# A fused model of six layers on one core: four edits to the order and the size of the work

## The reference

```
def routed_and_shared(x, cond):                  # 4096 tokens
    shared = (silu(x @ sw1.T) * (x @ sw3.T)) @ sw2.T          # hidden size 1024
    s = sigmoid(x @ router_w.T + cond @ router_t_w.T)         # 8 experts
    pick the 2 best of s + router_bias; gates = their s, normed to a sum of 1
    routed = sum over the 2: gate * gelu(x @ rw1[e].T) @ rw2[e].T   # hidden size 256
    return (shared + routed) / 3
def expert_ffn(y):                               # one expert of 8 for each batch,
    e = argmax(gelu(y[last token] @ Wp1 + bp1) @ Wp2 + bp2)   # chosen by its last row
    return y + 0.3 * ((gelu(y @ W1[e] + b1[e]) @ W2[e] + b2[e]) @ Wo + bo)   # hidden 1024
def hashed_ffn(x, token_ids, shift_state):       # 16 experts of 256 tokens by hash
    xk, xr = x mixed with the row before it
    return sigmoid(xr @ w_recept) * (relu(xk @ w_key[e]) ** 2 @ w_value[e])
def recurrent(x):                                # 32 steps, c = f * c + i * g
    gates from x @ w and c @ u; out = tanh(x @ wo + c_last @ uo + bo)

x = x + expert_ffn(routed_and_shared(x, cond))
x = x + recurrent(hashed_ffn(x, token_ids, cond))
```

## Time and profile before

| | us |
|---|---|
| runs (3) | 2507.08, 2508.03, 2508.68 |
| median | 2508.03 |
| profiled execution | 2510.33 |
| its span in the trace | 2508.7 |
| mean granted clock of TensorE | 0.994 |

### The profile page before, as it was taken

How to read it: one execution, slowest core, us unless ns; L and a number is a source line. 1 busy time by engine, 2 the same in 40 slices (tenths; PEclk the granted TensorE clock), 3 DMA queues, 4 the chain that set the end, 5 groups by cost and what they waited for, 6 DMA issues and landing times. The chain is left out here.

```text
span 2508.7 us, 40888 instructions
## 1 busy us (share of the span) xinstructions
PE 2456.5 (98%) x12556; PEld 2048.4 (82%) x12557; DVE 1148.4 (46%) x1766; ACT 896.8 (36%) x1454; POOL 548.5 (22%) x492
## 2 busy tenths in 40 slices
PE   8999999999999899999999989999999999999999
PEld 4778888888899688878888879989978888888877
DVE  5555555325343344334434357667643333333356
ACT  2233333226555222222222246666542222222234
POOL 1100000002222276656657510000001111111100
PEclk9999999999999899999999999999999999999999
DMA  7698898317466443363344265665641011110035
GB/s 283 212 344 305 300 319 318 136 48 264 151 241 222 167 122 110 116 248 108 110 154 150 84 240 218 237 241 215 234 155 42 26 34 29 29 34 25 25 99 186
DMA packets 134500, 412.81 MB, mean 165 GB/s; under 512 B 30115, under 2 KB 32611, under 8 KB 117778
## 3 DMA queue, kind: packets, MB, share of 16 engines
q1 hardware_dynamic: 107186, 315.25, 35.7%
q0 software_dynamic: 18736, 60.80, 8.0%
q10 hardware_dynamic: 8496, 35.69, 3.7%
HBM read 558.71 MB, written 144.80 MB: 280 GB/s over the span
## 5 line engine op out<-in xcount | busy, mean ns | idle before, releaser
L99 PE MATMUL s_g<-wx_hi,s_x_hi 128*128 128x512 f32 x512 | 203.4, 397 | 2.3 <-DVE s_x_lo L2268 1.6
L101 PE MATMUL s_g<-wx_hi,s_x_lo 128*128 128x512 f32 x512 | 200.2, 391 | 0.0
L100 PE MATMUL s_g<-wx_lo,s_x_hi 128*128 128x512 f32 x512 | 199.5, 390 | 0.0
L1981 DVE TENSOR_TENSOR s_w_lo<-s_w_raw,s_w_hi 128x1024 fp32r<-128x1024 f32 x124 | 146.5, 1222 | 75.2 <-ACT s_w_hi L1910 73.6
L99 PE MATMUL s_g<-s_u,s_c_hi 128*128 128x512 f32 x384 | 152.8, 398 | 1.6 <-PEq L1795 1.6
L101 PE MATMUL s_g<-s_u,s_c_lo 128*128 128x512 f32 x384 | 149.9, 390 | 0.0
L100 PE MATMUL s_g<-s_u,s_c_hi 128*128 128x512 f32 x384 | 149.5, 389 | 0.0
L99 PE MATMUL s_h_ps<-s_x_hi,s_w_hi 128*128 128x256 f32 x512 | 144.9, 283 | 1.7 <-DVE s_x_lo L2006 1.7
L100 PE MATMUL s_h_ps<-s_x_lo,s_w_hi 128*128 128x256 f32 x512 | 144.9, 283 | 0.0
L101 PE MATMUL s_h_ps<-s_x_hi,s_w_lo 128*128 128x256 f32 x512 | 144.9, 283 | 0.0
L2167 POOL DMA_INDIRECT s_y<-mid_hash_out,first_rec x32 | 31.5, 983 | 476.8 <-DMA mid_hash_out<-s_o 392.5
(11 more groups left out here) (401 smaller groups left out, 6913.9 us busy)
## 6 DMA issues: line engine op xcount, KB each, us to landing
s_half<-mid_w ACTq DMA_DIRECT2D x124, 2048.0 KB
s_w_raw<-in_w SPq DMA_DIRECT2D x64, 512.0 KB, 6.4
mid_w<-s_x_grp SPq DMA_DIRECT2D x32, 1024.0 KB, 5.6
mid_w<-s_pool_b SPq DMA_DIRECT2D x32, 1024.0 KB, 4.9
s_half<-mid_w SPq DMA_DIRECT2D x32, 1024.0 KB
s_w_raw<-in_w2h SPq DMA_DIRECT2D x16, 2048.0 KB, 7.5
s_w_raw<-in_w1h SPq DMA_DIRECT2D x15, 2048.0 KB, 7.5
mid_routed<-s_o_sb SPq DMA_DIRECT2D x72, 256.0 KB, 2.0
```

What stands on the lines that cost most here:

```text
L99: pe.matmul(out, a_hi, w_hi, start=first, stop=False, skip_group_check=True)
L100: pe.matmul(out, a_hi, w_lo, start=False, stop=False, skip_group_check=True)
L101: return pe.matmul(out, a_lo, w_hi, start=False, stop=last, skip_group_check=True)
L1981: dve.tensor_tensor(lo[:, c], raw[:, c], hi[:, c], ALU.subtract).then_inc(S[name + "_lo"], 1)
```

## The change

1. `places()` in the shared stage's DVE list moves from behind the parts that follow group 0 to ahead of the last of them.
2. `EARLY` is 4 instead of 5. ACT and DVE split the down weights of four experts at the end of the shared stage; the fifth is loaded and split in the routed stage, so that `LATE` has eight pieces, from step 2 to step 9, instead of six, from step 2 to 7. Each expert from number 5 on has its pieces two steps later.
3. `RT` is 71 instead of 72: the lists of 8 experts with 8192 places in all never need more than 71 whole tiles. All that runs over routed tiles is one shorter: gathers, matmuls, stores, and the lists of `places()` and `one_hots`. `CHECKED`, the counts at which the stage sees whether experts are through, ends with 71.
4. In the expert stage `combine` of batch j moves in DVE's list from ahead of `h_add(1)` of batch j - 1 to behind `h_lo(1)`. PE's list stays.

```
-RT = 2 * NTOK // P + ER
+RT = 2 * NTOK // P + ER - 1
-EARLY = 5
+EARLY = 4
 ...
@@ stage_shared, ACT
                     if g == G - 1:
                         routed_hi(m)
-                        if m == TG - 1:
-                            routed_hi(EARLY - 1)
@@ stage_shared, DVE
             x_lo(1)
             for point in range(HC, POINTS):
+                if point == POINTS - 1:
+                    places()
                 if is_part(0, point):
                     part_lo(part_at(0, point))
-            places()
@@ stage_ffn, POOL, gather
                 if isinstance(i, int) and i == 0:
                     for m in range(4):
-                        pool.wait_ge(R[f"o_out{m}"], 16 * RT // 4)
+                        pool.wait_ge(R[f"o_out{m}"], 16 * ((RT + 3 - m) // 4))
@@ stage_ffn, DVE
             software_pipeline(dve, NB, [
-                (2, z_add), (1, h_add(0)), (2, part_lo(z_lo, tz_ps, z_hi, "z_hi", "z_lo")), (0, combine), (1, h_add(1)),
-                (1, h_lo(0)), (2, x1_), (1, h_lo(1)), (3, hashed_lo(0, 2)),
+                (2, z_add), (1, h_add(0)), (2, part_lo(z_lo, tz_ps, z_hi, "z_hi", "z_lo")), (1, h_add(1)),
+                (1, h_lo(0)), (2, x1_), (1, h_lo(1)), (0, combine), (3, hashed_lo(0, 2)),
                 (3, xr_lo_), (2, last_mix), (3, hashed_lo(2, DC)), (0, make_shift),
                 (0, y_lo_)], 2)
```

More of the change, by code:

```diff
@@ L156, in stage_shared @@
                  "w_hi w_lo ones sig dve pe_rank ~rec_out zeroed ~zero_out ~route ~tile_in0 ~tile_in1 ~tile_in2 ~tile_in3 "
-                 "rw_in0 rw_in1 rw_in2 rw_in3 rw_in4 rw_hi "
+                 "rw_in0 rw_in1 rw_in2 rw_in3 rw_hi "
                  "xt_in xt_hi xt_lo gu silu hmul h_hi h_lo mm2 o_ready ~o_out0 ~o_out1 one_hot list_ps list_sum hash_members hash_total_read hash_rank_read "
@@ L848, in stage_routed @@
         ps = lambda n, s, t=FP32: ctx.enter_context(nc.psum_tensor("s2_" + n, s, t))
-        S = sems(nc, ctx, "s2_", "w_in5 w_in6 w_in7 w_hi w_lo wo_in0 wo_in1 wo_hi wo_lo tx x_hi x_lo mm1 "
+        S = sems(nc, ctx, "s2_", "w_in4 w_in5 w_in6 w_in7 w_hi w_lo wo_in0 wo_in1 wo_hi wo_lo tx x_hi x_lo mm1 "
                  "gelu th h_hi h_lo mm2 o_ready ~o_out0 ~o_out1 ~o_out2 ~o_out3 "
```

## The result

The changed kernel takes 2527.28 us at the median of four runs (2526.12 to 2531.51), the kernel before 2508.35 beside it: the ratio is 1.0079, 95% interval [1.0067, 1.0091], or 18.9 us slower. The direction was forecast, the size was not: 2516.0 was predicted, with a range that ended at 2523. The profiled execution took 2526.12 us with a span of 2524.5, 15.8 more than the span of before.

A forecast was written before the change was run, and what follows sets the result against it. TensorE, busy 98% of the span, was taken as the bound. Terms -1.7 - 1.2 - 1.7 - 3.4 + 4.0 + 10.0 - 4.8 + 6.8 gave +8.0 us, so 2516.0 us; range 2513 to 2522, or 2507 to 2523 with the held clock.

The forecast's parts named there:

- the -4.8 for step 14: Expert stage, after a 4 MB load: long step loses 6.3 us, y comes 1.5 later; bounds -6.3 and -2.
- the 0 for the steady steps: Expert stage, steps 4 to 31: receptance covers the later y with 0.2 us to spare, no loss.
- places(), -1.7: Shared stage: places() fits into VectorE's 11.21 us idle time, removing PE's 1.62 us wait; -1.7 us.
- The border: Shared to routed stage: four splits end it earlier, -1.2 us; less half clock behind it, -1.7 us.
- the late pieces: Routed stage: expert 7's pieces come late, waits of 2.7 and 1.3 us at up(7) and down(7); +4.0.
- The clock's term: Border: idle shrinks from 2.58 to 1.4 us, which no longer brings the clock down; -1.7 us.
- One tile fewer, -3.4: Routed stage: one step of x turns falls away with its gather and store; -3.4 us.
- The sum, steps 1 to 3: Expert stage: without receptance as cover, PE waits 4.4, 3.0 and 2.6 us for y; +10.0, half clocks +5.1.
- No more is late: Expert stage: gathers, blend and loads moved some 7 us later by the sum make nothing else late.
- the clock holds: Rival: the four new idles come but the granted clock stays; 2509.2 us, no change; chance 0.22.
- The early turns of y: Rival, the other side: earlier h_hi lets y arrive in time in steps 1 to 3; 2500.9 us; chance 0.12.
- The sum is late in every step: Rival: POOL runs beside the sum, 28 expert-stage steps lose 15 us in all; 2531 us; chance 0.06.

The follow-up runs named there:

- e12: Kernel before with places() moved, 71 tiles, ht in its old place, four early splits and late pieces from step 1: ratio 0.9984.
- e15: The changed kernel with the batch sum back in its old place: ratio 1.0002 to the kernel before.
- e4: Kernel before with four instead of five down weights split in the shared stage, nothing else: 1.0019, 4.8 us slower.
- e6: Kernel before with 71 routed tiles and 32 unused bytes that keep ht in its old place: 0.9982, 4.5 us faster.
- e1: Kernel before with an unused 32-byte tensor in front of ht_hi in the shared stage: 1.0012, 3.0 us slower.
- e3: Kernel before with only the batch sum moved behind h_lo(1): 1.0080, 18.5 us slower by the medians.
- e10: Kernel before with the sum behind h_lo(1) only from batch 4 on, in its old place for the first four: 1.0008.
- e8: e3 with ScalarE's issue of load_w2 moved behind h_hi(1): 1.0062, 15.5 us slower than the kernel before.
- e5: Kernel before with places() moved ahead of the last part, nothing else: 0.9987, 3.3 us faster.
- e16: e3 without POOL's indirect store of xk: 1.0065, 16.3 us slower than the kernel before.
- e13: Kernel before with an unused 128-byte tensor in front of ht_hi in the shared stage: ratio 1.0013.
- e14: Kernel before with places() moved, 71 tiles and ht 64 bytes behind its old place: 0.9968, 2500.22 against 2508.00 us.
- e9: Kernel before with an unused 64-byte tensor in front of ht_hi in the shared stage: ratio 0.9988.

## Why the prediction was wrong

Forecast were +8.0 us, measured +18.9. The step that failed is the sum over the moved batch sum, in two of its terms: the -4.8 for step 14, a price read off one execution, and the 0 for the steady steps, which rested on a spare of 0.2 us. A third miss, the place of ht in SBUF, was in no step at all.

- **places(), -1.7.** Right in mechanism, place and sign; measured -3.3 (-5.8 to -0.8). The idle time that it removes was 1.62 us in the profile of before and 0.8 to 2.8 in others, with half clock behind it in three.
- **The border, -1.2 and -1.7, and the late pieces, +4.0 with one half clock, +1.7.** Together +2.8; alone they measured +4.8 (+2.5 to +7.0). The waits are where the sum put them, 2.56 and 1.20 us for the forecast 2.7 and 1.3. The border's idle time is 1.52 us for 1.4. The clock's term is the uncertain one: behind 1.52 us it stayed at 1.00 in the changed kernel, in e12 and in e15, and fell for 3.4 us in e4.
- **One tile fewer, -3.4.** Its own worth is right (e6, -4.5 with an interval of -6.5 to -2.3). But "List matmuls of 142 instead of 144 columns are nothing beside it" stopped at instructions, and passed over memory: RT also sizes a tensor ahead of ht, and the move of ht by 32 bytes costs 3.0 us (+0.8 to +5.3, e1), 0.43 us in each of the eight groups by the traces. This term was missing from the sum and from its bounds.
- **The sum, steps 1 to 3: +10.0 and their clocks, +5.1.** Waits of 3.97, 2.86 and 2.42 us for the forecast 4.4, 3.0 and 2.6, and the same three half-clock stretches, the first 6.8 us long. The steps 1 to 4 are 13.9 us longer in e3, for the forecast 15.1: the mechanism and the size were right. e10 confirms that these steps are most of the loss. That the clock falls behind each of these waits is less sure than the prediction had it: behind 2.42 us it did in e3 and didn't in e8.
- **The sum, step 14: -4.8.** This is the term that failed most. The 25.06 us step belonged to the one profile at hand: of twelve profiles with the sum in its old place two have it (25.05 and 24.90 us), eight have 20.03 to 20.32, and two 21.2. With the sum late, that step and the one beside it are 19.83 and 19.89 us in the changed kernel, 39.7 together, against 43.8 in the profile of before, so that against this one profile 4.1 us do go, near the forecast. But in a usual execution they are 38.9 (20.08 and 18.78 in e5): there is nothing to win, and 0.9 us to lose. ScalarE's register load takes 0.95 us there (at 1094.5), and without POOL's indirect store (e16) only 0.3 of the 0.9 are left. The prediction noted that its profile lay 2.3 us above the median and didn't ask whether this step was in it. The bound of -2 was on the wrong side of nought.
- **The sum, steady steps: 0.** The spare of 0.2 us was read off the old order, in which the register load of the earlier trace rows's step was quick. With y 7 us later, POOL's blend and its indirect store come later too (its issue at 960.51, 3.05 us after ScalarE's z_hi; before it was 0.79 us ahead of it), and ScalarE's register load now falls 0.7 us behind the end of that issue and takes twice as long. 0.1 us in most of 23 steps adds up to 1.9 us in e3 (1.8 in the changed kernel), and the two steps about the second change of weights lose 0.6. The prediction did list what moves with the sum, POOL's queue among it, but only for what waits on it, not for what stands beside it. The clause "No more is late" was wrong by 0.3 us, and 0.2 was all there was; e8 and e16, each by another way, bring the 18.78 us back.

The sum again, with the expert stage by the traces of e3 and e1: 13.9 + 0.8 + 0.6 + 1.9 = 17.2 us (589.5 against 572.3), where the prediction had 10.0 + 5.1 - 4.8 = 10.3. That is 6.9 of the 10.9 us that were missed; the place of ht is 3.0, border and late pieces 2.0 beyond their terms, places() 1.6 and the tile 1.1 the other way. That makes 9.2; the rest is within what the intervals leave open, each of which is 2 us or more to either side.

Of the rivals, "the clock holds" did not come true: it fell behind all four new waits. The early turns of y waited, and the mechanism named for the other side was tried in e8: it takes 1.4 us off the wait in step 1 and nothing off those in steps 2 and 3, with less half clock 3.1 us in all, far from deciding. "The sum is late in every step" came true in most of the steps, with an eighth of its price (1.9 of 15 us) and by another mechanism: the sum's two instructions take 0.75 us at most in the changed kernel, and none of them has a POOL operation on tiles beside it; in the kernel before several have, and the first of the two took up to 1.88. By the Trainium skill's rule on the shared port (page "SBUF — State Buffer", section "Who interferes with whom") a DVE instruction with two SBUF inputs contends with a GpSimd instruction that reads SBUF. The rows agree: with none beside it, the sum isn't slowed.

## What to carry to other kernels

A gain that hangs on one long wait in one profile should be looked for in a second execution before it enters a sum; here it was there in two of twelve. When a count changes, ask which tensors it sizes and what lies behind them in SBUF: 32 bytes cost as much as a whole tile saved. And where a moved operation leaves less than half a microsecond to its reader, look at what else slides along with it on the other queues, register loads included.

## What the runs showed of the hardware

- **The pace of fp32r matmuls depends on where ht lies in SBUF.** Shifts of ht by -32, 0, +32, +64 and +128 bytes gave 66.57, 66.11, 66.54, 65.89 and 66.56 us for a group of 296 matmuls. Only the matmuls that have ht as an operand change, by a few ns each: from start to start they take 229.2 ns on average in the kernel before, 233.6, 233.5, 227.0 and 233.6 at the other four places, and the gate and up matmuls 227.4 or 227.5 at every one. A period of 64 or of 128 bytes is excluded by these; which rule there is stays open.
- **A register load can take twice as long behind an indirect store**: 0.53 to 0.54 instead of 0.27 us at the median on ScalarE, in e3, e10 and the changed kernel, where most of them start 0.5 to 0.7 us after POOL's issue ends. Over all eighteen profiles, of the 73 such loads that start 0.3 to 0.75 us after that end 66 take over 0.45 us; of the 400 that start more than 1 us after it one does. Without the store all 33 take 0.27. Which part of the store's traffic does it wasn't tried.
- **The same idle time of TensorE is followed by different clocks.** At the border of the first two stages 2.42 us of idle were followed by 3.4 us at half clock in e13 and e16 and by 6.8 in e10; 2.33 us by none (e1), 2.44 to 2.73 by 6.8 in six profiles and by 3.4 in one (2.55, e14), 2.86, 2.98 and 3.02 by 3.4, 6.8 and 6.8, in kernels whose work there is the same but for a few us. Elsewhere 2.50 us (e9, at 131.05) and 2.23 us (e14, at 1089.49) were followed by none. So the prediction's reading that 2.2 us or more always bring the clock down isn't borne out. At half speed 3.4 us cost 1.7 at most, so a border costs between nothing and 3.4 us on top of its idle time, which may be a part of why runs of the kernel before lie between 2504 and 2516 us; that wasn't measured.
